# A list scheduler whose clock waits for more, with new costs and group lengths

## The reference

```python
h = patches @ W.T + b                             # 768 -> 192
h = h + attn(layernorm(h))
h = h + moe(layernorm(h))

def attn(x):
    n = rmsnorm(x) * w_norm1
    z = (n @ W_in.T) * sigmoid(n @ W_gate.T)      # 384 channels
    dt_in, B, C = split(z @ W_xproj.T)            # 96, 16, 16
    dt = softplus(dt_in @ W_dt.T + b_dt)
    s[l] = exp(dt * -exp(A_log)) * s[l-1] + dt * z * B     # 16 states, along the 36 tokens
    x = x + (sum_states(s * C) + D_skip * z) @ W_out.T
    f = rmsnorm(x) * w_ffn_norm
    return x + (silu(f @ W_gate_ffn.T) * (f @ W_up.T)) @ W_down.T

def moe(x):                                       # 16 experts, 4 of them for each token
    t = rmsnorm(x) * scale
    weight = softmax(top4(t @ gate_w.T + gate_b))
    return x + sum_e(weight[e] * (swiglu(t @ w1[e] + b1[e]) @ w2[e] + b2[e]))
```

## Time and profile before

| | us |
|---|---|
| median of 3 runs | 626.79 (625.78 to 630.82) |
| the profiled execution | 627.44 |
| its span, first to last instruction | 625.6 |
| PE busy | 557.0 (89%) |
| DVE busy | 475.5 (76%) |
| POOL busy | 388.3 (62%) |
| ACT busy | 295.2 (47%) |
| mean granted TensorE clock | 0.945 of full |

### The profile page before, as it was taken

The page is one execution under the profiler, slowest core; times in us unless marked ns, Lnnn a source line. Parts: engine busy times, 40 slices in busy tenths (PEclk is TensorE's granted clock), DMA queues, the critical chain, the costliest instruction groups (busy, mean ns, idle before and its releaser), DMA issues.

```text
span 625.6 us, 10398 instructions
## 1 busy us (share of the span) xinstructions
PE 557.0 (89%) x3361; PEld 479.1 (77%) x3361; DVE 475.5 (76%) x897; ACT 295.2 (47%) x699; POOL 388.3 (62%) x447
## 2 busy tenths in 40 slices
PE   3959589977899999989999997999998889978896
PEld 3748478866698988879887885988886768857785
DVE  1166868889789789979879996999989556565664
ACT  1167846483544475544446474445442324323442
POOL 3257777767456458857555984767677355564674
PEclk9779959989899999999999997999999889997999
DMA  9993533432053343413343341554342266553781
GB/s 238 308 299 97 164 119 90 189 135 92 1 155 100 106 155 95 162 33 112 111 171 112 105 141 46 135 157 143 121 177 88 50 207 213 178 174 104 238 274 52
DMA packets 41827, 88.34 MB, mean 141 GB/s; under 512 B 9581, under 2 KB 34477, under 8 KB 35501
## 3 DMA queue, kind: packets, MB, share of 16 engines
q1 hardware_dynamic: 41772, 87.68, 43.4%
HBM read 77.24 MB, written 10.40 MB: 140 GB/s over the span
## 4 chain that ended last, share of the span: by engine, by line
PE 61%; DVE 15%; issue 6%; DMA 6%; ACT 5%; POOL 4%; SPq 2%; POOLq 0%; DVEq 0%; ACTq 0%
PE post L770 12%; PE y_sum L770 10%; PE sums L770 10%; PE gate_up L770 10%; PE pre L770 8%; PE linear_up L770 8%; DVE state L1255 4%; DMA w<-w_store 3%; PE fills L770 3%; DVE fills L1246 2%; DVE dts L1222 2%; SPq L709 1%; POOL read L1456 1%; DMA hid<-patches 1%; DVE scratch L1354 1%
## 5 line engine op out<-in xcount | busy, mean ns | idle before, releaser
L1456 POOL TENSOR_TENSOR read<-state,c_all 128x504 f32<-128x504 f32 (+1 forms) x120 | 147.0, 1228 | 83.2 <-DVE state L1255 54.8
L1255 DVE TENSOR_TENSOR_SCAN state<-a_bar,fills 128x504 f32<-128x504 f32 (+1 forms) x120 | 133.0, 1109 | 12.1 <-ACT a_bar L1035 4.1
L1485 POOL TENSOR_TENSOR scratch<-scratch 128x252 f32<-128x252 f32 (+1 forms) x120 | 81.6, 680 | 87.4 <-DVE scratch L1369 82.4
L770 PE MATMUL y_sum<-read,ident 128*128 128x252 f32 (+1 forms) x480 | 122.5, 382 | 4.1 <-POOL read L1456 3.7
L1035 ACT ACTIVATE scratch<-scratch 128x252 f32<-128x252 f32 (+1 forms) x120 | 47.3, 394 | 147.0 <-DVE scratch L1354 146.8
L770 PE MATMUL sums<-hid,w 128*128 128x252 f32 (+1 forms) x480 | 103.8, 377 | 4.8 <-POOL hid L1494 4.8
L770 PE MATMUL gate_up<-t_high,w 128*128 128x252 f32 (+1 forms) x360 | 89.3, 318 | 14.5 <-DVE route L1332 7.2
L770 PEld LDWEIGHTS y_sum<-read,ident 128*128 128x128 f32 x480 | 86.3, 201 | 19.8 <-issue 7.1
L1035 ACT ACTIVATE a_bar<-dts,decay 128x245 f32<-128x245 f32 (+1 forms) x240 | 100.2, 470 | 2.2 <-DVE dts L1230 2.2
L1494 POOL TENSOR_TENSOR hid<-scratch,route_rows 128x252 f32<-128x252 f32 (+1 forms) x120 | 84.9, 708 | 14.4 <-DMA route_rows<-mix_rows 7.6
L770 PE MATMUL linear_up<-t_high,w 128*128 128x252 f32 (+1 forms) x360 | 85.8, 308 | 2.3 <-ACT mix_w L1035 1.7
(11 more groups left out here) (166 smaller groups left out, 851.9 us busy)
## 6 DMA issues: line engine op xcount, KB each, us to landing
w<-w_store SPq DMA_DIRECT2D x40, 1152.0 KB, 5.7
route_rows<-mix_rows SPq DMA_DIRECT2D x192, 63.0 KB, 3.0
w_store<-w SPq DMA_DIRECT2D x8, 1152.0 KB, 5.0
scratch<-expert_w SPq DMA_DIRECT2D x16, 384.0 KB, 5.6
w<-expert_w SPq DMA_DIRECT2D x1, 2304.0 KB
route_rows<-mix_rows SPq DMA_DIRECT2D x48, 36.0 KB, 2.8
w_embed<-embed_w SPq DMA_DIRECT2D x3, 256.0 KB, 3.9
x_patch<-patches SPq DMA_DIRECT2D x1, 756.0 KB, 5.0
```

The lines of the kernel that those rows point to most:

```text
L770: return nc.tensor.matmul(out, lhsT, rhs, start=start, stop=stop, skip_group_check=shared, is_transpose=turned)
L1255: dve.tensor_tensor_scan(pair(state, i, c), pair(a_bar, i, c), pair(fills, i, c), 0.0, ALU.mult, ALU.add).then_inc(scanned.sem, 1)
L1456: pool.tensor_tensor(by_state(pair(read, i, c)), by_state(pair(state, i, c)), c_all[:, n:n + 2, 0:tok(c)], ALU.mult).then_inc(read_out.sem, 1)
L1485: pool.tensor_tensor(glu[:, 0:tok(c)], product[un % 2][:, 0:tok(c)], g_one[un % 2][:, 0:tok(c)], ALU.mult)\
```

## The change

`lay` now also waits, in its clock, for the end of every step that `needed` names; `needed` names drive for the first drive_b. Costs of 16 steps are changed. The fixed share of a cost is one number for each engine. The weight of waiting goes from 0.5 to 1.1. The lengths of the groups, one or two numbers before, are a number for each cut. Nothing else is touched.

```diff
+    if step == "drive_b" and i == 0:
+        return [(c, "drive", 0)]
...
+            for f in needed(c, step, i):
+                ready = max(ready, end.get(f, ended.get(f, 0.0)))
             for engine, us in COST[step]:
                 start = max(at[engine], ready)
...
-                at[engine] = start + us * (0.25 + 0.75 * size)
+                at[engine] = start + us * (FIXED[engine] + (1.0 - FIXED[engine]) * size)
...
-            places = spread_over(len(b), p, p + BEFORE_SPAN) + spread_over(len(s), p + 17.0, p + 24.0)
+            places = spread_over(len(b), p, p + BEFORE_SPANS[c]) + spread_over(len(s), p + 17.0, p + 24.0)
...
-        q = p + (AFTER_SPAN if c + 2 < NC else LAST_AFTER_SPAN)
+        q = p + AFTER_SPANS[c]
         posts += list(zip(a, spread_over(len(a), p, q)))
-        routed += list(zip(x, spread_over(len(x), q + 0.5, q + (EXPERT_SPAN if c + 2 < NC else LAST_EXPERT_SPAN))))
+        routed += list(zip(x, spread_over(len(x), q + 0.5, q + EXPERT_SPANS[c])))
...
+FIXED = {"P": 0.08, "V": 0.22, "S": 0.5, "G": 0.22}
 LATENCY = {"P": 0.22, "V": 0.12, "S": 0.1, "G": 0.14}
-WAIT_WEIGHT = 0.5
-BEFORE_SPAN = 15.5
-AFTER_SPAN, LAST_AFTER_SPAN = 20.9, 22.0
-EXPERT_SPAN, LAST_EXPERT_SPAN = 25.1, 21.7
+WAIT_WEIGHT = 1.1
+
+BEFORE_SPANS = (17.18, 25.79, 17.47, 14.74, 16.28)
+AFTER_SPANS = (24.46, 20.9, 20.9, 22.0, 22.0)
+EXPERT_SPANS = (21.86, 22.12, 22.6, 21.39, 36.17)
```

More of the change, by code:

```diff
@@ L342 @@
     "embed": (("P", .87),), "embedded": (("S", .9),), "mean": (("P", .85),), "center": (("V", .6),),
-    "square": (("S", .56),), "variance": (("P", .9),), "roots": (("V", .18),), "power": (("G", 1.),),
+    "square": (("S", 0.61),), "variance": (("P", .9),), "roots": (("V", .18),), "power": (("G", 1.),),
     "spread": (("P", .45),), "scale": (("V", 1.5),), "inproj": (("P", 1.7),),
-    "gate": (("S", .32),), "z": (("V", .38),), "xproj": (("P", 1.27),), "dt_in": (("S", .45),),
+    "gate": (("S", 0.37),), "z": (("V", .38),), "xproj": (("P", 1.27),), "dt_in": (("S", .45),),
     "bc_copy": (("V", .36),), "bc_high": (("S", .36),), "bc_low": (("V", .4),), "delta": (("P", .65),),
     "delta_abs": (("S", 1.2),), "delta_exp": (("S", .75),), "factor": (("S", .9),),
[L348 to L351, removed]
+    "poly": (("V", 0.9),), "log1p": (("V", 0.85),), "drive": (("G", 2.2),), "c_spread": (("P", .25),),
+    "c_copy": (("S", 0.57),), "decay": (("S", 0.8),), "fill": (("P", .25),), "drive_b": (("V", 0.62),),
+    "advance": (("V", 1.15),), "read": (("G", 1.26),), "collect": (("P", .85),), "y": (("V", .43),),
+    "outproj": (("P", 1.27),), "y1_add": (("V", .6),), "square2": (("S", 0.62),), "variance2": (("P", .9),),
     "roots2": (("V", .18),), "power2": (("G", 1.),), "spread2": (("P", .23),),
-    "scale2": (("V", .78),), "ffn_up": (("P", 1.7),), "ffn_tanh": (("S", .36),), "ffn_product": (("V", .78),),
+    "scale2": (("V", .78),), "ffn_up": (("P", 1.7),), "ffn_tanh": (("S", 0.37),), "ffn_product": (("V", .78),),
     "down": (("P", 1.7),), "h1": (("V", .55), ("G", 1.25)), "mean3": (("P", .85),), "center3": (("V", .58),),
@@ L358 @@
     "x_exp": (("S", .3),), "x_route": (("V", 1.2),), "x_turn": (("P", .25),), "x_mix": (("S", .7),),
-    "x_start": (("P", .85),), "x_gate": (("P", .6),), "x_linear": (("P", .6),), "x_min": (("V", .43),),
-    "x_tanh": (("S", .33),), "x_one": (("S", .4),), "x_low": (("V", .41),), "x_gated": (("V", .34),),
-    "x_glu": (("G", .68),), "x_scale": (("G", .68),), "x_down": (("P", .47),), "x_finish": (("V", 1.2),),
+    "x_start": (("P", .85),), "x_gate": (("P", .6),), "x_linear": (("P", .6),), "x_min": (("V", 0.44),),
+    "x_tanh": (("S", 0.38),), "x_one": (("S", 0.45),), "x_low": (("V", 0.43),), "x_gated": (("V", .34),),
+    "x_glu": (("G", 0.7),), "x_scale": (("G", 0.71),), "x_down": (("P", .47),), "x_finish": (("V", 1.2),),
     "split_w1": (("S", 1.), ("G", 2.)),
```

## The result

The changed kernel takes 632.59 us (median of 7 runs, 629.92 to 634.76) against 625.78 us for the kernel before (7 runs, 623.85 to 630.82). The ratio is 1.0103, with a 95% interval of 1.0066 to 1.0140: it is slower by 1%, where 617.7 us and faster was forecast. The time lies in the range, 1.4 us inside its slow end; the direction is the other one. The profiled execution took 632.59 us, its span 630.8, so it is 5.2 us longer than the one of before (span 625.6).

What follows compares the result with a forecast made beforehand. PE was taken as the bound wherever fed, so only idle PE and its clock could move. From 627.44 us, -9.8 - 3.1 + 3.8 = -9.1 gave 618.3 profiled, 617.7 as median; whole range 604 to 634.

Steps and rivals of the forecast that it cites:

- (a): The three seams between 137 and 400 us: half of 19.7 us of idle PE and lost clock comes back, -9.8.
- (b): 43 to 97 us, cut 0's scan beside cut 1's preparation: PE's waits shrink, -3.1 us, bounds 0 and -9.8.
- (d): After 474 us: 0, as cut 3's experts and cut 4's chain keep their places within 0.3 steps.
- (c): 97 to 137 us and the three full stretches: 0; 0 to 43: 0, a chain with little beside it.
- (e): Scan steps beside the seams at 48, 96 and 120 lack expert work for PE: +3.8 us, bounds 0 and 5.7.
- PE starves where the experts are missing: Rival, chance 0.20: PE lacks expert work beside the three seams of (e), nothing gained in (a) and (b), 635 us.
- The waits only move: Rival, 626 us: relieved queues meet the next wait, router chain stays serial; chance 0.26 together with the other no-change rival.
- The clock isn't what it says: Rival, about 627 us: x_gated beside the scan keeps half its mean cost, so little is gained; counted within no change's 0.26.
- the forecast's own range: 607 to 621 us for the whole kernel, with (a) between a third and nine tenths.

Runs made afterwards that it cites:

- e20: Kernel before with waits and costs, plus cut 0's after-scan length of 24.46 instead of 20.9: 628.28 us, 1.0048.
- e21: Kernel before with waits and costs, plus the new expert lengths alone: 635.31 us, 1.0163.
- e8: Changed kernel, but x_logits no longer waits for t_low in the planner's clock: 629.06 us, 1.0047 against the kernel before.

## Why the prediction was right and wrong

**The waits, (a) and (b): right in kind, about half in size.** Waits and costs were to bring 9.8 + 3.1 = 12.9 us and brought 7.3 (618.55 against 625.9). ScalarE's waits of c_all on read fell to 6.8 us by them, below the 12 that were foretold; the idle time of the three seams fell to 8.5 us, not to about 6. By place, in its profiled execution (8.9 us of span in all): 1.9 us are gained before the first scan step (42.3 against 44.2 us), where I had put nothing, next to nothing from there to the last y of cut 2, 4.4 us from it to the last y of cut 3 (273.6 to 384.1 us), and 2.2 behind the last y of cut 4, which (d) had put at nothing. (b) as such failed: 43 to 97 still idles 13.8 us.

**The clock.** At the last seam it was 0.89 with PE idle 3.27 us of 16, 0.78 with 3.71 in the kernel after, and 1.00 with 2.09 by waits and costs. The rule drawn on ahead (the Trainium skill, TensorE: Matmul & The Clock Gate, "Part 1: The HAM clock gate": activity lifts the throttled state) agrees with these three; at cut 3's seam, with 2.74 of 30 us idle, the clock came back only to 0.94.

**The costs: near enough.** They were given no term of their own. Alone they cost 0.44%; with the waits the two intervals lie over each other.

**(c), 0 to 43 at nothing: wrong.** I saw a chain with little beside it, and not that a step beside it can be put *into* it: a queue is in order, and a split_w1 ahead of square brings DRAM's delay into the chain and into SP's queue. That step is worth 0.24 to 0.38%, the whole head some 0.5%. Every order of the planner with the weight of 1.1 puts that split_w1 first, none with 0.5 does. The planner's `waits` counts PE and DVE alone; a split_w1 has steps on ScalarE and POOL only, never has a wait that counts, and so gains on the others as the weight rises.

**(d), after 474 at nothing: wrong, though not by its own sign.** From the last y of cut 4 to the end it is 144.7 us where it was 143.5, so the stretch after the last scan differs by 1.2 us and not by over 3. The loss lies around the end of that scan: +1.1 us at the last y of cut 3, +6.55 at the first x_linear behind the last seam, +5.2 at the end. I argued that cut 3's experts and cut 4's chain keep their places, and overlooked that the scan between them doesn't, since (e) had named 2.5 steps without experts ahead of that very seam, at 120.

**(e), given back +3.8, at most 5.7: the step that failed.** Weight and lengths cost 14.0 us on top of waits and costs (632.59 less 618.55) where +3.8 stood; the lengths by themselves cost 13.4 there (631.97, the change less the weight). I priced a step without experts at the PE time that goes empty in it. The runs show three things more. The units that leave these steps go ahead of the scan's own steps, which come late: in the kernel after the 13th step of cut 4's scan is 4.2 us late (436.6 against 432.4), 3.1 of them lost behind the last y of cut 3. The seam then opens on a late scan, so that the router chain waits as well (3.97 us at x_logits). And the clock falls in the empty steps (0.78 there). The loss adds up from cut to cut: in the trace of the change less the weight, against that of waits and costs, the last y of cut 1 is 0.7 us early, and those of cuts 2, 3 and 4 are 2.6, 7.3 and 9.9 us late. How much of it each of the three makes no run shows, and e20's 9.7 and e21's 16.8 us are no prices of the steps named in (e), since each shifts the end of cut 0's units as the change doesn't. For the weight (e) took no price at all, and the argument that a higher weight "prefers just the turns that keep PE fed" is refuted: it costs 2.3% alone, 3.9% on top of the waits and 2.9% on top of waits and costs (1.0163 against 0.9875), and nothing only beside the new lengths.

**The rivals.** "PE starves where the experts are missing" (635 us, at 0.20) comes nearest, with 632.6 measured, but in part by luck. It had the last seam, at 120, among its places, and its price was near because the parts offset each other. Its sign isn't there: at that seam PE idles 3.71 us where it idled 3.27, with DVE busy for 9.93 of 16 us and not over 95%, and half of the 1% hangs on the wait of x_logits (e8), which it doesn't name. "The waits only move" is what the table of waits shows in the kernel after (c_all on read 7.9 us less, on pre 13.1 more), but waits and costs alone show that they need not. "The clock isn't what it says" is refuted by the same run: the clock errs on x_gated there too, and 1.25% come.

**The range.** The low end of the forecast's own range, 607, doesn't come out of its terms: with (a) at nine tenths they give 627.44 - 17.7 - 3.1 + 3.8 - 0.65 = 609.8 us. Nothing else hangs on it. That 632.59 lies inside the whole range, whose high end was drawn at the starving case, says nothing for the sum.

**What stays open.** Why the weight and the lengths together (1.0103, on top of waits and costs) cost no more than the lengths do there without the weight (1.0107), and less than the weight without the lengths (1.0163): with the units shortened, leaving one's place sooner may put right what the lengths do. No run shows by which steps. Where the weight alone loses in 97 to 176 isn't traced to one step either. And any edit alters the planner's order in many places: the costs alone moved the time by 3.5 us without a wait or a place that was named ahead, so a difference of that size between two orders says little of its cause; those of over 2%, on which (e) rests, are larger.

## What to carry to other kernels

When a planner's model is corrected (it waits for what the program waits for, its costs are those of the trace), the constants that were tuned on the wrong model are not thereby in need of change: measure the correction alone first, and then each constant on top of it. A step that fills holes must be priced by what it displaces: taken from a few places, it crowds the others, and the chain that shares its queue comes late at the next hand-over (here 13.4 us, where at most 5.7 were counted). A cost function that counts the waits of some engines only will let steps on the others slip in front of a critical chain.

## What the hardware showed unexpectedly

How far an idle seam lengthens the work behind it. The same 12 matmul records of outproj took 2.79 us with waits and costs, and 4.72 us in the kernel after, both with nothing else on PE between them. The stretches ahead of and around them in the kernel after, and then around them with waits and costs (columns as in the earlier trace rows, the granted clock third from the end):

```profile
480.00:485.00 5.00, 2.10 (x6) 1.51 (x7) 2.55 (x5) 0.62 (x1) 4.31 (x4) 0.79 0.00 0
...
489.00:494.00 5.00, 5.00 (x16) 3.85 (x15) 1.32 (x7) 1.15 (x3) 0.00 (x0) 0.58 0.00 0
```

```profile
476.00:479.00 3.00, 3.00 (x17) 2.73 (x17) 2.32 (x15) 0.23 (x1) 2.04 (x2) 1.00 0.01 3
```

The clock is low where PE is full again, after a stretch in which it was busy for 2.10 of 5 us. The kernel before pays too: its first outproj, 6 records, takes 2.62 us at 0.59 (485 to 488 us), the second 1.44. All 12 stand ahead of x_turn in the kernel after, 2.1 us more than before, a third of the 6.55 us at the last seam.
